# Start of a sliding-window attention and mixture-of-experts layer: experts begun behind the gate product, the first combine weights spread by TensorE

## What is computed

```
h = relu(xn @ nm_w1 + nm_b1);  m = h @ nm_w2 + nm_b2
q, k, v = m @ q_w + q_b, m @ k_w + k_b, m @ v_w + v_b
attention: softmax(q k / sqrt(128)) v over the 65 keys around each token

scores = sigmoid(xn @ gate_w.T)                  # 16 experts
the 8 largest of scores + expert_bias are chosen; their scores,
divided by their sum and times 2.826, are the combine weights
y = sum over experts of weight * (silu(xn @ w_gate) * (xn @ w_up)) @ w_down
y += (silu(xn @ shared_gate) * (xn @ shared_up)) @ shared_down
out = x + attention + y
```

## Time and profile before

| what | us |
|---|---|
| median of 3 executions (lowest, highest) | 728.13 (727.63, 728.53) |
| the profiled execution | 727.74 |
| its span | 725.9 |
| TensorE busy | 705.1 (97% of the span) |
| VectorE / ScalarE / GpSimd busy | 574.0 / 439.1 / 400.5 |

### The profile page before, as it was taken

The page is one execution under the profiler, slowest core; times in us unless marked ns, Lnnn a source line. Parts: engine busy times, 40 slices in busy tenths (PEclk is TensorE's granted clock), DMA queues, the critical chain, the costliest instruction groups (busy, mean ns, idle before and its releaser), DMA issues.

```text
span 725.9 us, 10617 instructions
## 1 busy us (share of the span) xinstructions
PE 705.1 (97%) x3384; PEld 576.6 (79%) x3384; DVE 574.0 (79%) x1605; ACT 439.1 (60%) x874; POOL 400.5 (55%) x356
## 2 busy tenths in 40 slices
PE   5889999999999999999999999999999999999997
PEld 4667888788887888888788887888888788888886
DVE  5788788777888878788877888878787877888775
ACT  3575665656656565665656556566655656656573
POOL 3745555546565455555556564555565555655463
PEclk9999999999999999999999999999999999999999
DMA  7705316061240615215061240616225061430600
GB/s 254 258 5 169 110 30 220 29 233 44 95 184 2 232 45 182 96 46 215 18 234 44 110 168 4 231 45 200 78 50 221 8 234 45 127 137 7 243 1 15
DMA packets 36647, 84.72 MB, mean 117 GB/s; under 512 B 7152, under 2 KB 15472, under 8 KB 36592
## 3 DMA queue, kind: packets, MB, share of 16 engines
q1 hardware_dynamic: 36592, 84.05, 33.2%
HBM read 79.32 MB, written 4.72 MB: 116 GB/s over the span
## 4 chain that ended last, share of the span: by engine, by line
PE 79%; ACT 13%; DVE 4%; issue 2%; DMA 2%; POOL 0%; SPq 0%; DVEq 0%
PE ps_g L370 22%; PE ps_y L390 22%; PE ps_u L380 22%; ACT prob L553 4%; PE bank L306 3%; PE bank L348 3%; ACT L564 3%; ACT L528 2%; ACT silu L564 2%; PE bank L318 2%; PE bank L311 2%; DVE ps_u L889 2%; PE bank L329 1%; PE ps_y L357 1%; ACT h_hi L572 1%
## 5 line engine op out<-in xcount | busy, mean ns | idle before, releaser
L969 POOL TENSOR_TENSOR silu_c<-silu,comb_b 128x512 f32<-128x512 f32 x256 | 331.3, 1297 | 305.6 <-ACT silu L564 302.1
L572 ACT ACTIVATE h_hi<-ps_u 128x512 fp32r<-128x512 f32 x272 | 162.4, 597 | 267.3 <-DVE ps_u L889 267.3
L895 DVE TENSOR_TENSOR h_lo<-ps_u,h_hi 128x512 fp32r<-128x512 f32 x272 | 185.6, 682 | 59.9 <-ACT h_hi L572 59.6
L889 DVE TENSOR_TENSOR ps_u<-silu_c,ps_u 128x512 f32<-128x512 f32 x256 | 176.6, 690 | 50.3 <-PE ps_u L380 44.0
L564 ACT ACTIVATE silu<-ps_g 128x512 f32<-128x512 f32 x272 | 161.5, 594 | 0.2
L380 PE MATMUL ps_u<-xn_hi,exp_w_hi 128*128 128x512 f32 x272 | 110.7, 407 | 5.0 <-DVE h_lo L895 5.0
L390 PE MATMUL ps_y<-h_hi,exp_w_hi 128*128 128x512 f32 x272 | 112.6, 414 | 0.4 <-DVE h_lo L895 0.4
L370 PE MATMUL ps_g<-xn_hi,exp_w_hi 128*128 128x512 f32 x272 | 109.8, 404 | 2.1 <-ACT silu L564 0.6
L370 PE MATMUL ps_g<-xn_lo,exp_w_hi 128*128 128x512 f32 x272 | 108.0, 397 | 0.0
L370 PE MATMUL ps_g<-xn_hi,exp_w_lo 128*128 128x512 f32 x272 | 107.6, 396 | 0.0
L380 PE MATMUL ps_u<-xn_lo,exp_w_hi 128*128 128x512 f32 x272 | 107.4, 395 | 0.0
(11 more groups left out here) (139 smaller groups left out, 980.6 us busy)
## 6 DMA issues: line engine op xcount, KB each, us to landing
comb_b<-c_dram SPq DMA_DIRECT2D x64, 1024.0 KB, 8.5
xin<-x SPq DMA_DIRECT2D x16, 256.0 KB, 3.1
xres<-x_t SPq DMA_DIRECT2D x16, 256.0 KB, 2.6
out_t<-xres SPq DMA_DIRECT2D x16, 256.0 KB, 2.0
exp_raw<-wexp SPq DMA_DIRECT2D x3, 960.0 KB, 9.7
c_dram<-comb_t SPq DMA_DIRECT2D x64, 8.0 KB, 1.8
exp_raw<-wexp SPq DMA_DIRECT2D x1, 384.0 KB, 5.7
att_raw<-watt SPq DMA_DIRECT2D x1, 330.5 KB, 3.3
```

Of the source, the lines that this page charges most:

```text
L572: A(h_t[hbuf(par, s)][0][:], ps_u[(par + s) % 2][:], ACT.Copy).then_inc(s_h_hi, 1)
L889: V.tensor_tensor(ps_u[i][:], src[:], ps_u[i][:], ALU.mult).then_inc(s_h, 1)
L895: V.tensor_tensor(t[1][:], ps_u[(par + s) % 2][:], t[0][:].bitcast(F32), ALU.subtract)\
L969: G.tensor_tensor(silu_c[i][:].rearrange("p (l x) -> p l x", l=2), silu[i][:].rearrange("p (l x) -> p l x", l=2), comb_b[:, :, s1 - 1, :], ...
```

## The change

Everything that changes lies in the prologue and the first group; `when(g, s, fresh)` chooses the step `fresh` in the first group and `s` in all others.

- TensorE transposes xn tile by tile as VectorE makes the tiles. The hidden product, the score weights, the query product and the transposed hidden layer move out of the prologue: the queue is now gate product 0, hidden product, gate product 1, score weights, up product 0, gate product 2, and so on.
- The combine weights of experts 0 and 1 (`FRESH = 2`) no longer go through DRAM for the first group: TensorE transposes a column of `comb`, broadcast to a whole tile, four times for each of the two experts (`fresh_weights`), and ScalarE copies the result into `comb_b`. The first spread DMA brings experts 2 and 3 only.
- The first group's attention comes two steps later (xn of the next group: three), and so does the next group's routing, by one or two steps.
- The low parts of the step weights are GpSimd's but for steps 7 and 8 (`DVE_LO`), which stay on VectorE. GpSimd makes those of 0 to 3 in the prologue, and one behind each silu_c in slots 1 to 3 and 6 to 13.
- VectorE's prologue has the routing ahead of the wait for the score weights' side products. The step weights are loaded as five pieces (`EXPW`) in place of four; the expert bias is loaded behind x of the second group.

```
-EXPW = [(0, 2), (2, 7), (7, 12), (12, STEPS)]
+EXPW = [(0, 1), (1, 3), (3, 7), (7, 12), (12, STEPS)]
-EARLY = 8
+DVE_LO = (7, 8)
+FRESH = 2
...
+            def fresh_weights(e, dst):
+                for a in range(TILES):
+                    done = nc.tensor.transpose(dst[:, a * P:(a + 1) * P],
+                                               comb[:, a, e:e + 1].to_broadcast([P, P]), ident[:])
+                done.then_inc(s_fresh_mm, 1)
...
+                if first(g):
+                    if s == 0:
+                        score_weights()
+                    if s == 1:
+                        pe.wait_ge(S["comb"], 1)
+                        fresh_weights(0, bank[1])
+                        pe.wait_ge(s_vec2, 1)
+                        fresh_weights(1, bank[2])
+                    if s == 2:
+                        hid_turn(0)
+                        pe.wait_ge(s_scw, 1)
+                        pe.wait_ge(s_row, 1)
+                        pe.wait_ge(s_fresh, 1)
+                        q_proj(0)
...
+            def fresh_weights(e, src):
+                act.wait_ge(s_fresh_mm, e + 1)
+                A(comb_b[:, :, e, :], src[:].rearrange("p (l x) -> p l x", l=2), ACT.Copy).then_inc(s_fresh, 1)
...
+                if s == 3:
+                    expw_hi(5)
+                    expw_hi(6)
+                    expw_hi(7)
...
+                if s == 5:
+                    expw_hi(9)
+                    expw_hi(10)
+                if 8 <= s <= 13:
+                    expw_hi(s + 3)
...
-                if s == 3:
+                if s == when(g, 3, 5):
...
-                    if (s1 - 1) % CHUNK == 0:
+                    if first(g1) and s1 <= FRESH:
+                        pool.wait_ge(s_fresh, s1)
+                    elif (s1 - 1) % CHUNK == 0 or first(g1) and s1 == FRESH + 1:
...
+                if first(g) and (s in (1, 2, 3) or 6 <= s <= 13):
+                    expw_lo(s + 3)
```

More of the change, by code:

```diff
@@ L211, in first, with when @@
             return g == 0
+        def when(g, s, fresh):
+            return fresh if first(g) else s
         def last(g, ahead=0):
@@ L417, in prologue @@
                 pe.wait_ge(s_const, 1)
-                pe.wait_ge(S["xn"], 1)
-                turn(bank[1], flat(xn)).then_inc(S["xn_tp"], 1)
+                for a in range(TILES):
+                    if a < TILES - 1:
+                        pe.wait_ge(s_xn_tile, a + 1)
+                    else:
+                        pe.wait_ge(S["xn"], 1)
+                    done = nc.tensor.transpose(bank[1][:, a * P:(a + 1) * P], xn[:, a, :], ident[:])
+                done.then_inc(S["xn_tp"], 1)
                 pe.wait_ge(s_wt_in, 16)
@@ L455, in att_early @@
                     turn(bank[1], flat(xn)).then_inc(S["xn_tp"], 1)
-                if s == 3:
-                    if not first(g):
+                if s == when(g, 3, 5):
+                    if first(g):
+                        pe.wait_ge(s_fresh, FRESH)
+                    else:
                         pe.wait_ge(S["z_lo"], g)
@@ L460, in att_early @@
                     scores(0)
-                if s == 4 and more:
+                if s == when(g, 4, 6) and more:
                     pe.wait_ge(S["xn_lo"], g + 2)
@@ L626, in slot @@
                     h_hi(*before(g, par, s))
-                if s == 6:
+                if s == when(g, 6, 8):
                     prob_exp(g, 1)
+                if first(g) and s == 1:
+                    fresh_weights(0, bank[1])
+                    fresh_weights(1, bank[2])
                 if not (last(g) and s == STEPS - 1):
@@ L665, in normalise @@
                                            rstd[:, a:a + 1], ALU.subtract, ALU.mult)
+                    if first(g) and a < TILES - 1:
+                        done.then_inc(s_xn_tile, 1)
                 done.then_inc(S["xn"], 1)
@@ L861, in att @@
                         route_match(g + 1)
-                if s == 10:
-                    prob_lo(g, 1)
-                    if more:
-                        route_sum(g + 1)
-                if s == 11 and more:
-                    route_weights(g + 1, 1 - par)
-                if s == 12 and more2:
+                if s == when(g, 10, 12) and more:
+                    route_sum(g + 1)
+                if s == when(g, 11, 12) and more:
+                    route_weights(g + 1, 1 - par)
+                if s == when(g, 10, 12):
+                    prob_lo(g, 1)
+                if s == when(g, 12, 13) and more2:
                     moments(g + 2, par)
@@ L878, in att, with fresh_att @@
                         q_lo(g + 1)
+            def fresh_att(s):
+                if s == 0:
+                    score_weights()
+                if s == 1:
+                    hid_lo(0)
+                if s == 3:
+                    q_lo(0)
+                if s == 4:
+                    expw_lo(7)
+                if s == 5:
+                    expw_lo(8)
             def h_prod(g, par, s):
@@ L949, in prologue @@
                 inverse_std(0)
-                for s in range(EARLY):
+                for s in range(3):
                     expw_lo(s)
                 inverse_std(1)
+                expw_lo(3)
             def mask_terms(g, seq):
```

135 lines of the change are left out of this document (72 added, 63 removed).

## The result

| what | before | after |
|---|---|---|
| median (lowest, highest), us | 728.13 (727.52, 728.90), 9 executions | 726.19 (724.90, 727.19), 9 executions |
| the profiled execution, us | 727.74 | 725.87 |
| its span, us | 725.9 | 723.9 |
| TensorE busy, us | 705.1 | 707.0 |
| gate product of step 14, first group (the mark), starts at | 60.27 | 56.11 |

The changed kernel is faster: the ratio of the times is 0.9968, with an interval of 0.9959 to 0.9977 (the ratio on record; the two medians divided give 0.9973), 0.3% where 0.7% to 0.8% was forecast. The median of 726.19 lies 0.4 us above the top of the forecast range.

What follows compares the result with a forecast made beforehand. TensorE was taken as full behind the mark, GpSimd as pacing the first group: 21.35 + 28.4 work + 3.75 waits + 1.3 collisions put the mark at 54.9 instead of 60.27, so 727.74 - 5.4 = 722.3 us; range 720.2 to 725.8.

Steps and rivals of the forecast that it cites:

- Every us by which the mark moves moves the end: TensorE from the first group's gate product 14 on: no gaps, so 5.4 us at the mark shorten the whole time equally.
- later groups unchanged: Sign of being right, groups after the first: TensorE still busy 43.9 of 44 us.
- The sum of the first group: First group: silu_c(1) at 21.35, 28.4 us GpSimd work, 3.75 waits, 1.3 collisions; mark at 54.9 instead of 60.27.
- The clock's rise: TensorE, first group: upper clock level about 5 us into the dense run, at 18; until then 0.43 us a matmul.
- the split of step 5: GpSimd, first group: low part of step 5 waits 0.75 us for ScalarE, behind h(2), silu(4) and the query copies.
- the silu of step 9: GpSimd, first group: silu_c(9) waits 3.0 us for ScalarE's exponentials with their two table loads.
- the 1.3 us for collisions: First group: allowance for GpSimd and VectorE delaying each other, between 0 and 4.3 us, part for VectorE's xn tiles.
- Rival 3: TensorE's clock falls at the wait ahead of gate product 11 or rises later; costs 2.5 us, 724.8; 6%.
- Rival 2: VectorE's SBUF-only work blocked by busy GpSimd, three to five cases add 2.4 to 4 us: 724 to 726.5; 20%.
- Rival 1: First group: less waiting than summed, ScalarE or GpSimd have slack; mark 52.5 to 53.3, 720 to 720.8 us; 12%.
- Rivals 4 and 5: Group 1's weights late, 723.3 to 724.3, 3%; late score path makes steps 7 to 11 lose the gain, 727 to 729, 4%.
- Rival 6: First group: GpSimd's 21 operations and waits take 38.9 us, not 32.2; slower than before, 728.5 to 730; 3%.

Runs made afterwards that it cites:

- all seven kernels with the change: The kernel after and the six follow-up kernels built on it, all but the one that put only the swapped order into the kernel before; 720.91 to 731.73 us.
- the fourth experiment: Against the first experiment's kernel: combine weights of all 16 experts through DRAM again, without the early transposes and copies; 731.73 us, ratio 1.0043 to the kernel before.
- the first experiment: Against the kernel after: `prob_lo(g, 1)` again ahead of `route_sum` in step 10 of all groups but the first; 723.92 us, ratio 0.9950 to the kernel before.
- the third: Against the first experiment's kernel: nine unread matmuls on TensorE ahead of the wait for gate product 11, first group; 723.04 us, ratio 0.9934 to the kernel before.
- the last experiments: Against the first experiment's kernel: second group's xn moved to the end of VectorE's prologue, 722.74 us; the same with step 11's split made earlier, 720.91 us.
- sixth experiments: Against the first experiment's kernel: second group's xn made at the end of VectorE's prologue, not in step 2; 722.74 us, ratio 0.9923 to the kernel before.
- the second: Against the kernel before: only `route_sum` put ahead of `prob_lo(g, 1)` in step 10 of all groups but the first; 730.73 us, ratio 1.0031.

## Why the prediction was wrong, point by point

**The step that failed: "Everything that changes lies in the prologue and the first group".** The section on the change says so, and it is wrong. The prediction took it over: it carried the whole gain at the mark through to the end ("Every us by which the mark moves moves the end") and had "later groups unchanged", so that what the change costs in the later groups stood in its sum as nothing. `when(g, 10, 12)` keeps the step number of `route_sum` and `prob_lo` for the later groups, but the two blocks of code had changed places, so `route_sum` comes first in every group. That costs 0.14 us in each of 14 groups, 2.0 us in all, and has been shown from both sides. No rival of the prediction had a price for the later groups' own order. A comparison of VectorE's order in a later group would have shown it, and what such an operation costs beside `silu_c` could have been read in the trace of before, where `comb` took 0.22 us alone and 0.48 in a later group beside `silu_c`:

```profile
231.52 0.48 DVE L712 SCALAR_TENSOR_TENSOR comb<-weight,winv 128x64 f32<-128x64 f32 x1
```

**The mark that I watched did not see it.** "Later groups unchanged at 43.9 of 44" came out word for word, and the groups were still 0.14 us longer.

**The sum of the first group held.** What was 54.9 for the mark is 54.98 where the clock didn't fall. The hidden product's place, forecast at 12.93, is gate product 0's at 12.87. The first `silu_c` starts at 21.37 (21.35), the last step of `comb` at 15.39 (15.6), the third `silu_c` at 25.74 (25.2), waiting 0.88 us for its DMA, which landed 5.9 us after its issue. Up product 0 came at 17.91 and not at 19.4, without effect, since VectorE came to it only at 19.49, behind the score weights.

**The clock's rise at 17.9 us (forecast 18) is luck.** TensorE's queue is the same up to there in all seven kernels with the change, and begins gate product 0 at 12.70 to 13.06. But the first 128x512 matmul with only 0.23 to 0.24 us to the next starts at 16.11 in the fourth experiment and at 18.85 in the first. It mattered little: the mark is 54.98 in the first experiment, and 55.02 in the third, where the rise came 0.8 us earlier.

**Its terms were less exact than the sum.** GpSimd waited 1.23 us for the split of step 5 (0.75), since VectorE's xn tiles held up `h` of step 2, and 3.39 for the silu of step 9 (3.0). TensorE waited 1.27 us ahead of gate product 4 (1.7), 2.03 ahead of 5 (1.1) and 2.47 ahead of 11 (2.6), which began at 47.74 and not 46.6. It is here that most of the 1.3 us for collisions went: the xn tiles alone are 0.94 to 1.03 us by the last experiments. From gate product 11 to the mark the sum had 7.0 us, and the first experiment took 7.3 (47.67 to 54.98). The allowance was worked out from GpSimd's rows, though, and there it did not arise: of the nine low parts one took 1.34 us and the others 1.00 to 1.02, and no `silu_c` more than 1.30. The right total came in part by luck, since VectorE lost what GpSimd did not.

**Rival 3, the clock, came true in the profiled execution, and in others as far as the granted clock tells.** It had 6%, with 2.5 us as its price, because a wait of 2.67 us had no such effect in the trace of before. Eight matmuls ran at the lower level, 1.6 us, of which 1.13 reached the mark. One trace can't tell how often it happens. The times of the kernel after go with the mean granted clock: 724.90 at 0.999, 725.87 to 726.02 at 0.998, 726.19 to 726.52 at 0.997, 727.13 and 727.19 at 0.995. The Trainium skill, TensorE: Matmul & The Clock Gate, section "HAM oscillation — how this bites in real kernels", ties the half clock to pauses between bursts. The trace of the kernel after shows it behind a pause of 2.47 us; the traces of before (2.67 us) and of the first experiment (2.48 us) show no slow matmul behind theirs.

**The parts together.** The forecast of 722.3 us, 0.5 for the first experiment's lowest time against it (722.81), 2.1 for the order of two lines, and 1.3 from the lowest time of the kernel after to its median (726.19 less 724.90) are 726.2 us. That this closes is arithmetic and no check of its own, and the first experiment was timed in another series, whose kernel before was 0.5 us slower; what is shown by itself is the 2.1. The last term is not all new: the median of the kernel before is also 0.6 us above its lowest time (728.13 less 727.52).

**Rival 2** named the right mechanism at too high a price (2.4 to 4 us). VectorE was held up in four xn tiles of 2.09 us and not 1.08, which cost about 1.0 us at the mark, in `hid_lo` of 1.14, in one low part of 1.35, and in this pair, which took 2.35 us where it takes 0.52 to 0.67 in the second group:

```profile
47.65 2.35 DVE L890 TENSOR_SCALAR prob_n<-prob,row_inv 128x160 f32<-128x160 f32 x2
```

The pair stands on the way to the mark. In the first experiment, where it takes 2.36 us from 47.58 on, the chain that ends last runs from it over `h_lo`, the next product, its high part and the silu of step 12 to GpSimd and then to the mark:

```profile
52.65 1.30 POOL L1054 TENSOR_TENSOR silu_c<-silu,comb_b 128x512 f32<-128x512 f32 x1 [0.59 <-ACT silu L604]
...
54.98 0.50 PE L382 MATMUL ps_g<-xn_hi,exp_w_hi 128*128 128x512 f32 x1 [0.17 <-POOL exp_w_lo L1005]
```

The gate product of the mark stands 0.34 us later there than the matmul ahead of it would allow (54.41 and 0.23), which is the most that the pair can have cost. No run moved the pair, so this share is read from the rows and not tested.

**Rival 1** fell: there was no less waiting than summed. **Rivals 4 and 5** fell: TensorE has no wait for the weights of the second group and none for the scores. **Rival 6** fell for this kernel: GpSimd's queue did not take up the gain. In the fourth experiment, which starts the first `silu_c` 5.7 us later with the same queue, that queue does stop TensorE for 7.38 us, and the kernel is slower than before by 0.4%. But up to 4.8 us of its time are the clock's, so the queue alone is not shown to make it slower.

## What to carry to other kernels

When a step number is kept for the steady part of a loop, look whether the order inside that step is kept too: 0.14 us in each of 14 groups took back half of what the start had won. Compare the distance between like instructions from group to group and not only the busy share, since a delayed matmul overlaps its neighbours and looks busy. On VectorE put an operation that reads PSUM directly behind the long product and small ones with two SBUF inputs after it, when GpSimd still has a long instruction running; and give an engine that feeds TensorE its work in the time in which it waits anyway.

## What the runs showed of the hardware that I had not expected

- An operation on a small tile can cost more than twice as much when it starts beside a GpSimd instruction: `weight`, 128x64, 0.48 us against 0.21.
- Several such operations in a row take longer together: four xn tiles 2.09 us against 1.08. Before, the same four took 1.11 us alone (25.24 us, with GpSimd idle), so it is the neighbour that counts and not the place. Two tiles of 128x160 took 2.35 us beside GpSimd against 0.52 to 0.67.
- A pause of TensorE of about 2.5 us is followed by eight matmuls at the lower level in some executions and by none in others (eight after 2.47 us in the kernel after and in the fourth and sixth experiments; none after 2.48 us in the first, whose order on TensorE is the same, and none after 2.67 us in the kernel before and in the second). What decides between them stays open: only one execution of each kernel has a trace.
- Half the data didn't halve the time of the spread DMA: the 512 KB piece landed 5.9 us after its issue, where the whole first piece of before had taken 6.9.
- The clock's first rise is not fixed either: with the same queue it came between 16.1 and 18.9 us in the traces of the kernels with the change.
